# The last routed feed-forward layer adds its results to the stored output rows, and its router works on unscaled sums

## The reference

```python
def _forward(x, g1, g2, w_down, wq, wk, wv, w_up, router_w, w1, w2, w3):
    ...                                   # latent attention, 16 heads, o
    x = x + o @ w_up
    res = x
    t = _rmsnorm(x, g2).reshape(-1, D)    # x * g2 * rsqrt(mean(x*x) + 1e-5)
    probs = softmax(t @ router_w)         # 8 experts
    vals, idx = top_k(probs, 2)
    w = vals / sum(vals)
    gate = sum(one_hot(idx, E) * w[..., None], axis=1)
    hid = silu(einsum('td,edf->tef', t, w1)) * einsum('td,edf->tef', t, w3)
    y_e = einsum('tef,efd->ted', hid, w2)
    return res + einsum('ted,te->td', y_e, gate)
...
x = x + tanh(g_ffn[3]) * _L3_ffn_ref(_layernorm(x), ...)
return x
```

## Time and profile before

| | us |
|---|---|
| median of 3 runs | 3182.34 (3182.22 to 3183.45) |
| the profiled execution | 3179.92 |
| its span (first to last recorded work) | 3178.6 |
| TensorE busy | 3011.6 |
| end of the last head's products for the router | 2892.8 |
| first transposes of the first routed chunk | 2920.38 |
| last copy of a routed result | 3152.16 |
| last addition to x | ends 3176.83 |

### The profile page before, as it was taken

How to read it: one execution, slowest core, us unless ns; L and a number is a source line. 1 busy time by engine, 2 the same in 40 slices (tenths; PEclk the granted TensorE clock), 3 DMA queues, 4 the chain that set the end, 5 groups by cost and what they waited for, 6 DMA issues and landing times.

```text
span 3178.6 us, 43530 instructions
## 1 busy us (share of the span) xinstructions
PE 3011.6 (95%) x16332; PEld 2211.4 (70%) x16332; DVE 2116.0 (67%) x3869; ACT 1225.1 (39%) x2357; POOL 859.9 (27%) x1308
## 2 busy tenths in 40 slices
PE   8999999999999999999999999899999899997996
PEld 6778777677767776777699999665567655555664
DVE  7996788558855885686478887783328677764113
ACT  5343333552354335432233333441225356662331
POOL 3207301100100020001246556440433231112554
PEclk9999999999999999999999999999999999998998
DMA  7000100010002000200032222003650011113533
GB/s 192 15 1 1 56 1 1 14 60 10 0 14 69 1 1 14 68 1 1 14 91 83 80 80 67 21 1 106 225 190 1 30 34 46 33 38 123 204 125 109
DMA packets 104614, 176.42 MB, mean 56 GB/s; under 512 B 27125, under 2 KB 75799, under 8 KB 99671
## 3 DMA queue, kind: packets, MB, share of 16 engines
q1 hardware_dynamic: 89527, 102.32, 10.5%
q0 software_dynamic: 14880, 71.33, 6.4%
HBM read 198.31 MB, written 17.56 MB: 68 GB/s over the span
## 4 chain that ended last, share of the span: by engine, by line
PE 75%; DVE 14%; issue 4%; ACT 2%; DMA 2%; POOL 1%; SPq 1%; DVEq 0%; ACTq 0%; POOLq 0%
PE psum L424 9%; PE psum L447 8%; PE psum L1444 7%; PE psum L1456 6%; PE psum L2578 6%; PE psum L1925 5%; PE psum L1880 5%; PE psum L2599 3%; PE psum L1164 2%; PE psum L414 2%; PE psum L460 2%; PE psum L2754 2%; PE psum L3179 2%; DVE psum L3437 1%; PE psum L3199 1%
## 5 line engine op out<-in xcount | busy, mean ns | idle before, releaser
L424 PE MATMUL psum<-Vt,shared 128*128 128x256 f32 (+1 forms) x1600 | 362.1, 381 | 0.4
L447 PE MATMUL psum<-Kt,xnTt 128*128 128x512 f32 (+1 forms) x960 | 343.8, 508 | 0.6 <-ACT xnTt L537 0.6
L424 PEld LDWEIGHTS psum<-Vt,shared 128*128 128x128 f32 (+1 forms) x1600 | 298.1, 190 | 39.6 <-issue 1.5
L447 PEld LDWEIGHTS psum<-Kt,xnTt 128*128 128x128 f32 x960 | 179.9, 190 | 158.0 <-issue 154.1
L245 POOL TENSOR_SCALAR root_v<-meanvar 128x8 f32<-128x8 f32 (+3 forms) x19 | 8.6, 454 | 904.2 <-DVE meanvar L223 904.2
L1456 PEld LDWEIGHTS psum<-expert_w,prep 128*128 128x128 f32 x1024 | 194.6, 190 | 77.7 <-issue 57.4
L3437 DVE CUSTOM_DVE_ANT_0 psum<-psum,expert_w 128x128 f32<-128x128 f32 (+7 forms) x256 | 191.8, 775 | 76.6 <-PE psum L3179 73.5
L1456 PE MATMUL psum<-expert_w,prep 128*128 128x256 f32 x1024 | 240.8, 379 | 0.0
L1444 PE MATMUL psum<-weights,expert_w 128*128 128x512 f32 x512 | 240.3, 593 | 0.0
L1370 DVE SCALAR_TENSOR_TENSOR bias<-Kt,small,bias 128x1232 f32<-128x1232 f32 x96 | 149.1, 1554 | 129.8 <-ACT Kt L1354 128.5
L3326 ACT ACTIVATE prep<-psum 128x512 f32<-128x512 f32 (+3 forms) x384 | 167.3, 494 | 108.7 <-PE psum L3202 107.8
(11 more groups left out here) (516 smaller groups left out, 6691.8 us busy)
## 6 DMA issues: line engine op xcount, KB each, us to landing
weights<-in_L_ffn_w SPq DMA_DIRECT2D x32, 512.0 KB, 4.8
expert_w<-in_L_ffn_w SPq DMA_DIRECT2D x32, 512.0 KB, 4.7
expert_w<-in_L_xattn_Wf SPq DMA_DIRECT2D x16, 512.0 KB, 5.7
weights<-q_parts SPq DMA_DIRECT2D x32, 144.0 KB
weights<-k_parts SPq DMA_DIRECT2D x96, 48.0 KB
weights<-in_L_xattn_Wk SPq DMA_DIRECT2D x4, 1024.0 KB, 4.9
weights<-in_L_xattn_Wv SPq DMA_DIRECT2D x4, 1024.0 KB, 8.4
weights<-in_L_xattn_Wq SPq DMA_DIRECT2D x4, 1024.0 KB, 5.3
```

The source lines that it names most:

```text
L424: ins = pe.matmul(o_bank(t), probT[0:rows, t % 2, c, :], Vt[0:rows, t // TB, c, :], start=(c == 8), stop=(c == 7))
L447: ins = pe.matmul(flat[:, par * 3 * BANK + at:par * 3 * BANK + at + cols], xnTt[:, par, k, :], Kt[:, t // TB, k, src:src + cols], start=(k ...
```

## The change

Four parts of L3 are changed, and the order in which POOL and DVE work through a chunk list. Where the diff leaves lines out, most are waits of DVE and POOL on their own last instruction.

1. Output rows: SP stores x (with tanh(g) * inner added) into the output in two halves as soon as each is complete (`sp_summed`). POOL's scatter of a chunk then goes to the output itself, with `compute_op=ALU.add`. Because a token's two results go to the same row, a scatter waits until the one before has landed. Padding entries go to 256 extra rows ahead of the output, which SP fills with the identity once.
2. Weights of the sum: DVE multiplies a second product by its slot's gate while copying it. The gate reaches the slot with the row: SP stores the two gates of each token behind its row in HBM (`L3_rows` is 258 wide), and `gate_of` picks one by `choice`. POOL makes the gates (`pool_gates`) between the first three weight fetches and the first row fetches.
3. The router takes the unscaled sums: G turns `inner`, not the scaled rows, and the choice is made on unscaled logits. The statistics of batch 1 are squares summed on ACT; ACT scales batch 1's rows, behind its copy of the counts. The difference of the two best logits is multiplied by the root afterwards.
4. The 23 idle matmuls ahead of G go, and those behind the last L become 37 instead of 14.
5. POOL's order in a pass becomes: rows of c + 3, scatter of c, weights of c + 4 (L3 only). `dve_tokens` makes `token_row` ahead of `result_row` (both layers).

```diff
-    L2_rows, L3_rows = ([scratch(f"{layer}_rows", (NT * P, D)), scratch(f"{layer}_results", (2 * P + K_ * NT * P, D))]
-                        for layer, K_ in (("L2", 1), ("L3", 2)))
+    L2_rows = [scratch("L2_rows", (NT * P, D)), scratch("L2_results", (2 * P + NT * P, D))]
+    L3_rows = scratch("L3_rows", (NT * P, D + 2))
...
+        if r == 1:
+            then(dve, dve.tensor_scalar(choice[:, :, 1], v, float(2 * P + NT * P), None, ALU.is_ge))
+            then(dve, dve.scalar_tensor_tensor(v, choice[:, :, 1], -float(NT * P), v, ALU.mult, ALU.add))
+        then(dve, dve.tensor_scalar(g, v, -float(2 * P), 0.0, ALU.add, ALU.max))
+        dve.tensor_copy(token_row[:, 0:total], g).then_inc(tokens_made, 1)
...
-            then(dve, dve.tensor_scalar(g, v, float(2 * P + NT * P), -float(NT * P), ALU.is_ge, ALU.mult))
-            then(dve, dve.tensor_tensor(v, g, v, ALU.add))
-        then(dve, dve.tensor_scalar(v, v, -float(2 * P), 0.0, ALU.add, ALU.max))
-        dve.tensor_copy(token_row[:, 0:total], v).then_inc(tokens_made, 1)
+            then(dve, dve.tensor_scalar(choice[:, :, 0], choice[:, :, 1], -1.0, 1.0, ALU.mult, ALU.add))
+    GATED = 3
+    def pool_gates(pool):
+        pool.wait_ge(gating_back, 4)
+        pool.tensor_scalar(root_v[:, :], rank[:, :], 1.0, None, ALU.add).then_inc(pool_step, 1)
...
+        pool.tensor_tensor(root_w[:, :], root_v[:, :], minus_half[:, :], ALU.pow).then_inc(pool_step, 1)
...
+        pool.tensor_tensor(root_w[:, :], root_w[:, :], root_w[:, :], ALU.mult).then_inc(pool_step, 1)
...
+        pool.tensor_tensor(root_v[:, :], root_v[:, :], root_w[:, :], ALU.mult).then_inc(pool_step, 1)
...
+        pool.tensor_scalar(root_v[:, :], root_v[:, :], -1.0, 2.0, ALU.mult, ALU.add).then_inc(pool_step, 1)
...
+        pool.tensor_tensor(root_w[:, :], root_w[:, :], root_v[:, :], ALU.mult).then_inc(pool_step, 1)
...
+        pool.tensor_scalar(gates[:, :, 0], root_w[:, :], tanh_g[:, 7:8], None, ALU.mult).then_inc(pool_step, 1)
...
+        pool.tensor_tensor(gates[:, :, 1], gates[:, :, 0], rank[:, :], ALU.mult).then_inc(bo_added, 1)
...
+        landing = gated_rows_in if r == 1 else rows_in
...
-            pool.indirect_dma_start(rows_in[:, c % 3, :], None, x_rows,
+            pool.indirect_dma_start(landing[:, c % 3, :], None, x_rows,
...
+        if r == 1:
+            pool_gates(pool)
...
-        pool.wait_ge(rows_stored, 32 * (r + 1))
+        pool.wait_ge(rows_stored, 32 if r == 0 else 32 + 48)
...
+                if r == 1:
+                    pool.wait_ge(gating_product, GATED + c + 1)
                 fetch_rows(c + 3)
-            if c + 4 < total:
+            if c + 4 < total and r == 0:
...
-            if c >= 2:
-                pool.wait_ge(results_sent[(c - 2) % 3], 16 * uses_before(r, (c - 2) % 3, c - 1, 3))
-            pool.indirect_dma_start(y_rows, bass.IndirectOffsetOnAxis(result_row[:, c:c + 1], 0),
-                                    y_out[:, c % 3, :], None).then_inc(results_sent[c % 3], 16)
+            if r == 0:
+                if c >= 2:
+                    pool.wait_ge(results_sent[(c - 2) % 3], 16 * uses_before(r, (c - 2) % 3, c - 1, 3))
+                pool.indirect_dma_start(y_rows, bass.IndirectOffsetOnAxis(result_row[:, c:c + 1], 0),
+                                        y_out[:, c % 3, :], None).then_inc(results_sent[c % 3], 16)
+            else:
+                if c == 0:
+                    pool.wait_ge(out_stored, 16 * 4)
+                else:
+                    pool.wait_ge(results_sent[(c - 1) % 3], 16 * uses_before(r, (c - 1) % 3, c, 3))
+                pool.indirect_dma_start(y_rows, bass.IndirectOffsetOnAxis(result_row[:, c:c + 1], 0),
+                                        y_out[:, c % 3, :], None, compute_op=ALU.add).then_inc(results_sent[c % 3], 16)
+                if c + 4 < total:
+                    pool.wait_ge(routed_second, base + c + 1)
+                    fetch_weights(c + 4)
...
-            sp.dma_start(x_rows[b * S:(b + 1) * S].rearrange("(t p) d -> p t d", p=P),
+            sp.dma_start(x_rows[b * S:(b + 1) * S, 0:D].rearrange("(t p) d -> p t d", p=P),
...
-    def sp_results(sp, r, y_rows):
-        sp.wait_ge(rows_stored, 32 * (r + 1))
-        if r == 1:
-            sp.wait_ge(inner_added, 1)
+    def sp_results(sp, y_rows):
+        sp.wait_ge(rows_stored, 32)
...
-            sp.wait_ge(results_sent[s], 16 * uses_before(r, s, TOTALS[r], 3))
+            sp.wait_ge(results_sent[s], 16 * uses_before(0, s, TOTALS[0], 3))
...
-            for k in range(r + 1):
-                at = P * (2 + k * NT + q)
...
-                             y_rows[at:at + 4 * P].rearrange("(t p) d -> p t d", p=P)).then_inc(back_landed[q // 4], 16)
+            at = P * (2 + q)
+            sp.dma_start(inner[:, q:q + 4, :],
+                         y_rows[at:at + 4 * P].rearrange("(t p) d -> p t d", p=P)).then_inc(back_landed[q // 4], 16)
...
-            dve.tensor_copy(y_out[:, c % 3, :], psum[:, 6 + c % 2, 0:D]).then_inc(routed_copied, 1)
+            if r == 1:
+                dve.wait_ge(gating_product, GATED + c + 1)
+                dve.tensor_scalar(y_out[:, c % 3, :], psum[:, 6 + c % 2, 0:D], slot_gate[:, c % 2:c % 2 + 1], None,
+                                  ALU.mult).then_inc(routed_copied, 1)
+            else:
+                dve.tensor_copy(y_out[:, c % 3, :], psum[:, 6 + c % 2, 0:D]).then_inc(routed_copied, 1)
+        def gate_of(c):
+            if c >= 1:
+                dve.wait_ge(gating_product, GATED + c)
+            if c >= 2:
+                dve.wait_ge(routed_copied, base + c - 1)
+            then(dve, dve.tensor_tensor(of_choices, gated_rows_in[:, c % 3, D:D + 2], choice[:, c, :], ALU.mult))
+            dve.tensor_tensor(slot_gate[:, c % 2:c % 2 + 1], of_choices[:, 0:1], of_choices[:, 1:2],
+                              ALU.add).then_inc(gating_product, 1)
...
-                sp_rows(sp, 1, send3, range(1), L3_rows[0])
-        sp_rows(sp, 1, send3, range(1, 2), L3_rows[0])
-        sp_results(sp, 1, L3_rows[1])
-        for t in range(NT):
-            if t % TG == TG - 1:
-                sp.wait_ge(bo_added, 2 * NT + t // TG + 1)
-            else:
-                sp.wait_ge(x_final, t - t // TG + 1)
-            sp.dma_start(out[t // TB].rearrange("(t p) d -> p t d", p=P)[:, t % TB, :], x[:, t, :]).then_inc(out_stored, 16)
-        sp.wait_ge(out_stored, 16 * NT)
+                sp_rows(sp, 1, send3, range(1), L3_rows)
+        sp_summed(sp, 0)
+        sp_rows(sp, 1, send3, range(1, 2), L3_rows)
+        sp.wait_ge(bo_added, 2 * NT + 1)
+        sp.dma_start(L3_rows[:, D:D + 2].rearrange("(t p) k -> p t k", p=P), gates[:, :, 0:2]).then_inc(rows_stored, 16)
+        sp_summed(sp, 1)
+        for s in range(3):
+            sp.wait_ge(results_sent[s], 16 * uses_before(1, s, TOTALS[1], 3))
+    def sp_summed(sp, b):
+        sp.wait_ge(x_final, b + 1)
+        at = 2 * P + b * S
+        sp.dma_start(out[at:at + S].rearrange("(t p) d -> p t d", p=P), x[:, b * TB:(b + 1) * TB, :]).then_inc(out_stored, 16)
...
-            pe.wait_ge(rows_ready, NT + TB * b + 2 * i + 2)
+            pe.wait_ge(step_taken, taken(STEP_AT["Y", b, i]))
...
-                                       send3[:, TB * b + 2 * i + t, k * P:(k + 1) * P], ident[:, :])
+                                       inner[:, TB * b + 2 * i + t, k * P:(k + 1) * P], ident[:, :])
...
-            if u == STEP_AT["G", 1, 0]:
-                pe_stay_at_work(pe, psum[:, 6, :], 23)
...
-        pe_stay_at_work(pe, psum[:, 7, :], 14)
+        pe_stay_at_work(pe, psum[:, 7, :], 37)
...
-        act.wait_ge(gating_product, 3)
-        act.activation(wide[:, 0], wide[:, 0], ACT.Exp).then_inc(gating_back, 1)
+        act.wait_ge(step_taken, taken(STEP_AT["Y", 1, 3]))
+        for t in range(TB, NT):
+            ins = act.activation(send3[:, t, :], inner[:, t, :], ACT.Square, scale=float(D) ** -0.5,
+                                 accum_out=meanvar[:, t, 1:2])
+        ins.then_inc(variance_made, 1)
...
+        act.wait_ge(root_made, ROOTS)
+        for t in range(TB, NT):
+            act.mul(send3[:, t, :], inner[:, t, :], rstd[:, t:t + 1]).then_inc(rows_ready, 1)
+        act.wait_ge(gating_product, GATED)
+        act.activation(rank[:, :], rank[:, :], ACT.Exp).then_inc(gating_back, 1)
...
+            if b == 1:
+                return
...
+                if h == HEADS:
+                    ins = dve.scalar_tensor_tensor(x[:, j, :], inner[:, j, :], tanh_g[:, 7:8], x[:, j, :], ALU.mult, ALU.add)
...
-        for u in range(46, 52):
-            dve_step_of(dve, u)
-        dve_mean_square(dve, 1)
-        dve.wait_ge(root_made, dve_roots())
-        for i in range(4):
-            dve_sent_rows(dve, 1, i)
-        for u in range(52, len(LATENT_STEPS)):
+        ins.then_inc(x_final, 1)
+        for u in range(46, len(LATENT_STEPS)):
...
-        p, first_, second_, left = (wide[:, n] for n in range(4))
```

(21 more changed lines are left out.)

64 lines of the change are left out of this document (23 added, 41 removed).

## The result

| | before | after |
|---|---|---|
| median of the runs, us | 3179.04 (9 runs, 3172.14 to 3183.45) | 3173.31 (9 runs, 3163.16 to 3174.82) |
| span of the profiled execution | 3178.6 | 3172.5 |

The ratio is 0.9976, with an interval of 0.9968 to 0.9985: about 7.6 us faster by the ratio (the medians themselves differ by 5.7). The forecast was 3159, with 3151 to 3171 as its range. So the kernel got faster, but by a third of what was expected, and the time lies above the range.

The account below looks back on a forecast made before the run. TensorE was taken to bound the kernel (95% busy), except in the last layer's tail and router. Span 3178.6 - 21.8 - 5.9 + 2.6 + 1.5 = 3155.0; from the median, 3182.34 - 23.6 = 3158.7, stated as 3159, range 3151 to 3171.

Parts of the forecast that it names:

- the loop: Last layer's chunk passes: period stays 5.82 us, later weights may show in three bursts; 1.5 us added, bounds 0 and 9.
- the start: Router to first routed chunk: first rows reach TensorE at 2914.5 against 2920.38, 5.9 us gained, bounds 3.4 and 8.
- the tail: After the last routed copy: fetching back and adding leave, the last adding store takes 3.5 us; 21.8 us gained.
- Rival (2): Loop bursts: stores land over 5.5 us after issue and delay successors, weights and rows; 6 to 9 us more, 3166; chance 0.15.
- Rival (4): Loop: an adding store takes more than a period; at 8 us latency the loop costs 95 us, 3253; chance 0.09.
- Rivals (1): First chunk: gates' store lands at 2909, gap under 2 us, clock full; 8 us gained at the start, 3154; chance 0.18.
- (5): Loop: adding store's latency is 6.0 to 6.3 us, so the time stays within 0.2%; chance 0.03.
- Rival (3): First chunk: gates late (2917) and a long low clock, 10 us as in the router's gap; 3163.5; chance 0.12.
- the worst bound: Gates' store before the first row fetch: all 2 us of its small pieces come behind the weights, landing at 2913.
- The clock: First chunk: a 3.7 us TensorE gap behind the idle matmuls lowers the granted clock; 2.6 us charged.

Follow-up runs that it names:

- e1: Kernel after, with the scatter overwriting output rows instead of adding, pass order unchanged: 3159.51 us in one run, loop 240.9.
- e2: Kernel after, still adding, with GpSimd's pass order back to weights, store, rows: 3161.92 us, ratio 0.9948 to the kernel before, loop 236.3.
- e7: Kernel after, with a plain overwriting store and the pass order back to weights, store, rows: 3158.82 us in one run, loop 234.2.
- e4: Kernel after, with gates made ahead of the first weight fetches and stored ahead of the second half of scaled rows: 3165.31 us, ratio 0.9968.
- e6: Kernel after, with 50 idle matmul calls behind the token search in place of 14: 3167.91 us in one run, loop 243.7.
- e5: Kernel after, with pass order store, rows, weights, so rows are asked for ahead of weights: 3163.07 us, ratio 0.9948, loop 236.9.
- e9: Kernel after: rows before weights, early gates, 20 idle calls before counts and behind tokens, third chunk's weights behind all three first row fetches: 3152.73 us, ratio 0.9924.
- e10: Kernel after: pass order weights, store, rows; early gates, 20 idle calls before counts and behind tokens, third chunk's weights behind first three row fetches: 3150.87 us, 0.9919.
- e8: Kernel after: rows before weights, early gates, 20 idle calls before counts and behind tokens, third chunk's weights behind the first row fetch: 3152.15 us, ratio 0.991.
- e11: Kernel after, with rows stored 256 wide, gates in their own scratch and ones multiplied in; second execution: 3163.86 us, loop 243.9.

## Why the prediction was right in its direction and wrong in its size

The sum was -23.6; the span gave -6.1. Of the 17.5 between them 12.1 are the loop, 5.2 the start, 1.4 the tail, less 1.3 that came ahead of T.

**The loop is the step that failed.** The prediction said of the weights' 1.3 us: "There the 1.3 us may show: 0 to 1.3 us in each of three bursts", and took 1.5 us with 9 as upper bound. Measured are 13.6: 10.0 us more of waits for rows, 1.6 us of low clock behind the longest of them, and about 2 us by which the passes with a wait are longer than the wait itself tells (0.2 us each). It priced a delay of the weights, which are used some 11 us after they are asked for, and not what the new order does to the rows, which are used after 6. Of the rows it said "Row fetches keep their place". Before, rows were asked for 2.63 us behind the weights; after, 1.34 us. The weights themselves moved from 0.78 to 2.68 us behind the copy, since a store stands ahead of them whose issue takes 1.6 us and not 1.0. The rows moved by only 0.6, so they find 1.3 us more of a 3.6 us transfer (an estimate: 1.57 MB at the 433 GB/s of the earlier trace rows) still ahead of them. The profile before had the warning. The transfers that it issued from 2938 to 2942, with the time from issue to landing in us:

```profile
weights<-in_L_experts,prep POOLq DMA_INDIRECT x1, 7.2
L_results<-shared,prep POOLq DMA_INDIRECT x1, 6.2
shared<-L_rows,prep POOLq DMA_INDIRECT x1, 5.1
```

Issued at 2938.84 and 2941.50, weights and rows landed at 2946.0 and 2946.6: the rows right behind the weights. Their use came 6.05 us after their issue (2947.55), so there was under 1 us of slack here, and none where rows took 6.6 us. Beyond that slack each microsecond of queueing is paid in full, in the passes of the bursts.

The square of e1, e2, e7 and the kernel after puts prices on it, the clock taken out: the order costs 5.2 us with a plain store and 9.5 with an adding one; adding costs 2.9 us in the order of before and 7.2 in that of after. Together they cost 4.3 us more than the sum of both alone. These are single executions, and three loops alike (after, e4, e6) differed by 1.8 us, or 4.3 before the clock is taken out. That undoing the order alone brings back most of the loss (9.5 of 12.0 us) is shown by e2, and again by e5; that the order and the adding make each other dearer is likely, but rests on one execution of each corner.

**Rival (2)**, the chain of stores with "6 to 9 us more: 3166", was nearest in time. But its mechanism is not the one that acted: in the kernel after only the very last store waited for its predecessor. It appears in e2, where all waits of TensorE together are 2.9 us. Rival (4) is refuted: an adding store takes 3.9 us in the median (e2, e4, e5, e9, e10) and the period outside bursts stays 5.82, as forecast. Rivals (1) and (5) are out as well. Rival (3) had the gates late and a long low clock, and both came true: the lower level was granted for about 10 us, 2915 to 2925.2. It cost 2.6 us only, since TensorE stood idle for the first 3.5 us of it.

**The start.** G without its idle gap, the counts released by the idle matmuls near 2890, gates and not tokens ahead of the row fetch, and the low clock in the first chunks: all as forecast. Sizes, counted from T: counts 0.8 us later (the 37 idle calls took 10.1 us at a clock of 0.83, not 8.5), the gates 1.6 us longer (7.0 us and not 5.3: the power took 3.73 us here, and 2.92 in e4, where it ran earlier), the row fetch 3.4 us later behind the gates' store (7.9 us to its landing and 0.8 to the fetch, against 5.3), the rows 0.5 faster: 5.2 together. For the store, "at worst all 2 us of them come behind the weights" was the true case and the worst bound still too low: 7.9 us from issue, against 4.5 in e4 with no weights ahead of it (4.1 forecast). The difference, 3.4 us, is what the weights ahead of it cost.

The Trainium skill's rule of alternating packets ("DMA: Bandwidth & Descriptors", "Queues, rings and completion order") gave an estimated 6.3 us from issue to landing if the gates travel in a dozen packets per engine, and the worst bound, 7.3 us, with one packet per piece. Between 2906 and 2916 the trace has 3102 packets with 1.06 MB on the hardware queue, which is one for each of the 2048 pieces and some 1000 for the 1 KB rows of the output store. Whether an engine takes several of them at one turn it doesn't show. The measured 7.9 us are nearer to one per piece, and 0.6 us over even that.

**The clock** cost 2.6 us at chunk 0 as predicted, although the gap was 8.3 us and not 3.7, and in e4, behind a gap of 3.30 us, it cost 2.2. e6 shows that it is the gap. That the number fits is partly luck: the clock fell inside the gap and not after work resumed, and the sum had no term for the 1.6 us inside the loop.

**The tail** gained 20.4 of 21.8: the store takes 3.85 us and not 3.5, twice, and between a landing and the next store pass 0.75 us that the prediction left out. The Trainium skill's page on the cost of the fold ("Collectives: The Full Stack", "The bandwidth ceiling: the fold count and why AG ≠ RS ≠ AR") gave an estimated 0.3 us over a plain store. Measured are 1.3 to 1.4 (2.5 in e1, 3.85 after), both from the start of the issue, which itself is 0.6 us longer. The measurement decides: a single adding store of 128 KB is dearer than that estimate, and what in it takes the time is not shown.

## What to carry to other kernels

When instructions of one queue are reordered, price the urgent transfer by what stands ahead of it when it is asked for, not the moved one by its own delay: between weights used 11 us after they are asked for and rows used after 6, 1.3 us less distance cost 9.5 us, and 1.6 more by the clock. Most of a removed tail of 20 us can be given back in a loop whose transfers had under 1 us of slack; test the new tail (adding stores) and the new order apart, as only the first was needed: with weights first, early gates, fewer idle matmuls and the third chunk's weights behind the first rows (e10) it gave 26 us and not 7.6. Idle matmuls that keep the clock up must be counted again whenever what they cover moves: 37 of them held back counts that DVE had ready nearly 6 us before, and none covered the gap that had opened.

## What the runs showed of the hardware

- An adding scatter of 128 rows of 1 KB takes 1.61 us of GpSimd's issue against 1.01 for a plain one, 96 packets more, and 3.85 us against 2.5 from issue to landing; with weights of the pass before still in flight 5.04 us (2939.71 to 2944.75 in the chain of the kernel after).
- 2048 pieces of 8 bytes are as many packets in the trace: 3.9 to 4.5 us to landing with no weights ahead (e4, e8, e9, e10), 7.1 to 7.9 behind three fetches of weights (after, e1, e2, e5, e6, e7).
- Indirect transfers on GpSimd's queue landed in the order in which they were asked for, the rows 0.6 us behind the weights (before, 2946.0 and 2946.6). Rows asked for 1.34 us behind 1.57 MB of weights came 7.5 us after issue; 4.98 us behind them, in 3.7 (e2).
- The same power of 128x16 on GpSimd took 2.92 us in four kernels with early gates and 3.73 in those where it ran later, beside DVE's long one-hots. That these slow it was not tested.
- A wait of 2.0 to 2.35 us inside the loop was followed by a stretch at the lower clock in the kernel after, e1 and e6 (1.6 to 1.7 us lost each), but one of 2.15 us in e2 was not.
- The clock is granted differently to like work. The same 74 idle matmuls took 8.51 us in e2, e4 and e11 and 9.85 to 10.14 in five others, and one whole execution ran at 0.684.
